# Down products and projection of a first layer as token rows instead of transposed sums, with its bias added on GpSimd and the recurrence begun one pair of chunks sooner

## The chip, the cores and the metric

One core of a Trainium2 chip. The time is device time of one execution of the kernel, in microseconds (us), as the median of three runs. Lower is better.

## The reference

Input is `x` of 4 sequences of 512 tokens, 256 wide; on the chip the tokens are taken in blocks of 128 per sequence, so that 4 blocks of 4x128 tokens make up the work. Two layers follow each other, each a mixer and a mixture of experts beside it, added to the residual:

```python
xn = _layernorm(x)
x = x + _L0_attn_ref(xn, w_qkv, w_proj, b_proj) + _L0_ffn_ref(xn, ...)
xn = _layernorm(x)
x = x + _L1_attn_ref(xn, W_in, b_in, W_out, b_out, gamma, beta) + _L1_ffn_ref(xn, ...)
```

- First mixer: linear attention in 8 heads. `q` and `k` pass a relu, `v` is padded with a column of ones, `vk = v_pad k^T` is summed over all tokens of a sequence, `vk q` is divided by its last row, and `@ w_proj.T + b_proj` closes it.
- First mixture: 16 experts of 176 hidden units, the top 6 by softmax for each token. The kernel computes all 2,816 hidden units for all tokens, in 22 chunks of 128, and multiplies each by the token's weight for its expert, which is 0 for the ten others.
- Second mixer: a recurrence over the 512 tokens, `s = tanh(u_t + s * gamma + beta)` with 512 hidden values, where `u = xn @ W_in.T + b_in`; its states go through `W_out`.
- Second mixture: 8 experts of 176 hidden units, the top 2 for each token with weights that sum to 1, and a shared expert of 352 hidden units.

## The kernel before

Matrices are split in a head and a tail in float16, and a product is three matmuls (`PRODUCTS`: head by head, tail by head, head by tail) into one float32 sum. TensorE's unit of work is a matmul of 128x128 weights with 512 moving columns: 4 sequences x 128 tokens.

**Stages.** A prologue makes the first norm, the attention's sums over tokens and the first pieces of weights. Then come four phases, one for each block of tokens, in which the 22 chunks of the dense mixture pass in 11 pairs (`pair(k, ...)`, `PAIRS`). For each chunk TensorE makes the gate product into bank G, the up product into a bank of U (6 matmuls each), and the down product of the chunk two before (`down`, L1020, 6 matmuls) into the two banks Y of the phase's parity. ScalarE makes the silu (L1328) and the head of the hidden units (`hh`, L1336), VectorE multiplies (L1845) and weighs (L1851), GpSimd makes the tail (`hl`, L1984). G is one bank, so the gate of the next chunk waits for the silu of this one.

**Side work.** Each engine runs a written list. `stages(phase)` gives two tables: `front[k]`, side work that stands in front of pair k, and `woven[k]`, parts that VectorE puts between its own operations of pair k. So, in phases 1 to 3, for the block before: the sums leave the banks (front 1 and 2), the second layer's norm is woven into pairs 2 and 3, `norm_turn` transposes its result (front 4), `logits` stands in front 5, the products `inputs` with `W_in` in fronts 5 and 6 (constants `INPUT_A`, `INPUT_B`). For the own block, `project` (`w_proj`, L848 on) adds to the same sums (front 2).

**Sums of the first layer.** `down` has weights as the stationary operand and hidden units as the moving one, so its sum has the features on partitions and tokens along the columns: `Y[j % 2][dh]`, half `dh` of the features. Before the sums can be added to the residual `xres`, which has tokens on partitions, ScalarE copies them with scale and bias to `yT` (`sum_copy`, L1242), TensorE transposes 8 squares of 128 (`sum_turn`, L889) and VectorE adds (L1697).

**The recurrence.** It runs beside all this: a step is a scan on VectorE (L1830) and a tanh on ScalarE (L1368), each waiting for the other. From `FIRST_TICK` of phase 1 on, a pair carries 12 steps (`STEPS`). Its inputs are copied from the banks into the buffer RING by ScalarE (`input_copy`, L1263). In the first phases RING also holds staged pieces of the second layer's weights, of which `PAIR_PIECES` gives the pair: (1, 2) holds pieces 38 to 41. When piece 40, the last of the sorted gate and up weights, is done on ScalarE (heads, L1205) and VectorE (tails, L1491, L1493), SP issues the DMA that parks them in DRAM (`park`, L709), behind loads of later pieces (`load_down`, L684). `input_copy(0, 0)` and `input_copy(1, 0)` wait for a parking:

```python
def input_copy(j, c, bank_):
    act.wait_ge(u_done, KH * j + c + 1)
    if j < 2 and c == 0:
        act.wait_ge(parked_out[j], 16)
```

**The units.** Behind the phases come 35 units (`UNITS`): 3 of the shared expert, 23 of pairs of tiles with tokens sorted by expert, 9 shared. `UNIT_STEPS` says how many steps of the recurrence each carries, `UNIT_FRONT`, `UNIT_GAPS` and `UNIT_WOVEN` what side work: the last block's sums and norm among the first, its routing and scatter after, and from unit 18 the gathers of routed results (L2033) with stores of tiles (L2052) on GpSimd's queue.

## Time and profile before

| | |
|---|---|
| three runs, median (lowest to highest) | 658.88 us (658.23 to 660.16) |
| profiled execution, span from first to last instruction | 655.6 us |
| profiled execution, its own time | none recorded beside the span |
| TensorE, matmuls, busy | 610.9 us |
| VectorE busy | 447.3 us |
| ScalarE busy | 366.1 us |
| GpSimd busy | 239.1 us |
| mean granted clock of TensorE | 0.990 |

The span does not hold what lies before the first instruction and after the last. Of the stages, phases 0 to 3 begin at about 55, 152, 258 and 360 us, the units at about 460. Engines are named PE (TensorE), PEld (its weight loads), DVE (VectorE), ACT (ScalarE), POOL (GpSimd) and SP (SyncE). Two consecutive starts of a row of matmuls tell the time of one better than the column of durations, which overlap. A bracket at the end of a row gives the idle time of the engine ahead of it, and what ended it.

### The profile page before, as it was taken

To read this page: it belongs to the slowest core of one execution; us is meant where nothing else is said; L and a number is where in the kernel's file an instruction comes from. 1 tells how busy PE (TensorE), PEld (TensorE's weight loads), DVE (VectorE), ACT (ScalarE), POOL (GpSimd) and SP (SyncE) were. 2 spreads that over 40 slices of the span, in tenths; PEclk is the share of its full clock that TensorE was granted. 3 is DMA by queue.
4 is the path that set the end of the run, shared out by engine and by line. 5 is a ranking of instruction groups with operands and counts; after the bars stand their busy time and mean duration, and the time that the engine had idled before them with its cause. 6 is when DMAs were issued, how large, how long until landed. Compare 5 with 4: busy or idle time off the path is not lost. (4 is left out here: it accounts for less than half of the span.)

```text
span 655.6 us, 12530 instructions
## 1 busy us (share of the span) xinstructions
PE 610.9 (93%) x3579; PEld 338.7 (52%) x3579; DVE 447.3 (68%) x1526; ACT 366.1 (56%) x1004; POOL 239.1 (36%) x256
## 2 busy tenths in 40 slices
PE   5999899999999999999999989999979989777997
PEld 2665444544444444444454434454446667556675
DVE  7983967667862677776478696477676666676677
ACT  2446345456546446657755657754546765663561
POOL 5246222132242225524224533222542361374371
PEclk8999999999999999999999999999998999999999
DMA  8203667872386452855346650324512445563143
GB/s 298 80 1 105 224 222 252 274 237 78 112 325 216 140 185 84 270 194 192 127 155 202 217 179 30 128 94 71 112 51 66 101 135 115 129 174 110 66 129 97
DMA packets 89548, 97.99 MB, mean 149 GB/s; under 512 B 29375, under 2 KB 80159, under 8 KB 89055
## 3 DMA queue, kind: packets, MB, share of 16 engines
q10 hardware_dynamic: 45472, 46.01, 21.4%
q1 hardware_dynamic: 38734, 36.82, 19.1%
q0 software_dynamic: 5280, 14.42, 7.0%
q8 instruction: 29, 0.48, 0.3%
q14 instruction: 33, 0.26, 0.1%
HBM read 27.96 MB, written 63.24 MB: 139 GB/s over the span
## 5 line engine op out<-in xcount | busy, mean ns | idle before, releaser
L1984 POOL TENSOR_TENSOR hl<-scr,hh 128x512 f16<-128x512 f32 (+2 forms) x91 | 105.3, 1157 | 276.6 <-ACT hh L1336 276.6
L1368 ACT ACTIVATE RING<-zbuf 128x16 f32<-128x16 f32 x512 | 110.9, 217 | 148.5 <-DVE zbuf L1830 143.5
L762 PE MATMUL G<-xT,W 128*128 128x512 f16 (+2 forms) x600 | 145.9, 379 | 8.2 <-ACT scr L1328 5.7
L762 PE MATMUL U<-xT,W 128*128 128x512 f16 (+2 forms) x600 | 145.8, 379 | 2.8 <-DVE scr L1845 2.8
L1830 DVE TENSOR_TENSOR_SCAN zbuf<-C,RING 128x32 f32<-128x32 f32 x354 | 77.8, 220 | 75.0 <-ACT RING L1368 74.6
L762 PEld LDWEIGHTS U<-xT,W 128*128 128x128 f16 (+3 forms) x600 | 60.9, 102 | 71.9 <-DVE scr L1845 4.3
L762 PEld LDWEIGHTS G<-xT,W 128*128 128x128 f16 (+3 forms) x600 | 60.1, 102 | 73.1 <-issue 6.4
L1020 PE MATMUL Y<-hh,W 128*128 128x512 f16 x352 | 90.3, 379 | 0.0
L1851 DVE TENSOR_TENSOR U<-U,CS 128x512 f32<-128x512 f32 x88 | 60.4, 686 | 38.6 <-PE U L762 31.9
L1328 ACT ACTIVATE scr<-G 128x512 f32<-128x512 f32 (+2 forms) x100 | 58.9, 589 | 45.0 <-PE G L762 44.5
L1336 ACT ACTIVATE hh<-scr 128x512 f16<-128x512 f32 (+2 forms) x100 | 61.8, 618 | 29.1 <-DVE scr L1845 28.9
L1845 DVE TENSOR_TENSOR scr<-scr,U 128x512 f32<-128x512 f32 (+2 forms) x100 | 67.4, 674 | 3.0 <-PE U L762 0.9
L1020 PEld LDWEIGHTS Y<-hh,W 128*128 128x128 f16 (+1 forms) x352 | 34.4, 98 | 41.5 <-issue 0.3
L1020 PE MATMUL Y<-hl,W 128*128 128x512 f16 x176 | 52.4, 379 | 0.3 <-POOL hl L1984 0.2
L1830 DVE TENSOR_TENSOR_SCAN zbuf<-gam,RING 128x32 f32<-128x32 f32 x158 | 35.6, 225 | 24.6 <-ACT RING L1368 24.2
L2052 POOL DMA_DIRECT2D yrows<-scr x46 | 25.7, 559 | 59.1 <-issue 58.5
L2033 POOL DMA_INDIRECT W<-yrows,row_id x32 | 34.0, 1061 | 11.2 <-issue 6.7
L2020 POOL DMA_INDIRECT xrows<-XR,row_id x32 | 34.4, 1074 | 8.0 <-issue 7.7
L762 PE MATMUL Y<-xT,W 128*128 128x512 f16 x144 | 33.2, 379 | 1.8 <-DVE gexp L1516 1.8
L1020 PEld LDWEIGHTS Y<-hl,W 128*128 128x128 f16 (+1 forms) x176 | 16.6, 98 | 22.3 <-POOL hl L1984 3.7
L952 PE MATMUL U<-W,xT 128*128 128x512 f16 x96 | 25.0, 399 | 2.7 <-DVE W L1503 2.7
L1503 DVE SCALAR_TENSOR_TENSOR W<-stage,W 128x768 f16<-128x768 f32 (+1 forms) x21 | 20.6, 1003 | 7.4 <-ACT W L1183 7.0
(204 smaller groups left out, 839.5 us busy)
## 6 DMA issues: line engine op xcount, KB each, us to landing
xrows<-zeros ACTq DMA_DIRECT2D x13, 1280.0 KB, 5.7
yrows<-zeros ACTq DMA_DIRECT2D x10, 1536.0 KB, 6.0
stage<-weights SPq DMA_DIRECT2D x20, 384.0 KB
yrows<-zeros ACTq DMA_DIRECT2D x5, 1408.0 KB, 6.0
yrows<-scr POOLq DMA_DIRECT2D x46, 128.0 KB
xrows<-zeros ACTq DMA_DIRECT2D x5, 1152.0 KB, 5.4
stage<-weights SPq DMA_DIRECT2D x14, 256.0 KB
parked<-RING SPq DMA_DIRECT2D x1, 3520.0 KB, 12.0
```

The source lines that it names most:

```text
L762: last = nc.tensor.matmul(bank_, w(wp), act(ap), start=start and n == 0, stop=stop and n == count - 1)
L1020: last = nc.tensor.matmul(Y[j % 2][dh][:, :], weight(CHUNK0 + c, wp, 2 * KD * P + dh * P), act[ap][:, a, :], start=start and m == 0, stop= ...
L1328: nc.scalar.activation(sg[a][rows, :], G[rows, :], ACT.Silu, scale=1.0 / W_SCALE).then_inc(silu_done, 1)
L1336: nc.scalar.activation(hh[rows, a, :], h32[a][rows, :], ACT.Copy).then_inc(hhead_done, 1)
L1368: nc.scalar.activation(RING[:, (t + 1) % RING_T, ::2], zbuf[:, 1::2], ACT.Tanh).then_inc(state_done, 1)
L1830: nc.vector.tensor_tensor_scan(zbuf[:, :], held_gamma if held else gam[:, :], RING[:, t % RING_T, :], 0.0, ALU.mult, ALU.add)\
L1845: nc.vector.tensor_tensor(h32[a][rows, :], sg[a][rows, :], U[a][rows, :], ALU.mult).then_inc(gated_done, 1)
L1851: nc.vector.tensor_tensor(U[a][:, :], U[a][:, :], spread_slot(phase), ALU.mult).then_inc(weighed_done, 1)
L1984: nc.gpsimd.tensor_tensor(hl[rows, a, :], h32[a][rows, :], hh[rows, a, :], ALU.subtract)\
L2020: nc.gpsimd.indirect_dma_start(xrows, bass.IndirectOffsetOnAxis(row_id[:, j, b, k:k + 1], 0), XR[:, b, :], None).then_inc(scattered, 16)
L2033: nc.gpsimd.indirect_dma_start(YG[:, i % RING_YG, :], None, yrows, bass.IndirectOffsetOnAxis(row_id[:, j, b, k:k + 1], 0))\
L2052: nc.gpsimd.dma_start(yrows[DS(row, P), :], yT[r % 2][:, t * DIM:(t + 1) * DIM])\
```

## The change

- `down` and `project` exchange the operands: 128 tokens of hidden units are stationary and 256 features of the weights move. A down is 12 matmuls of 256 columns for 6 of 512; the sums are rows of tokens, the halves of `Y[j % 2][b // 2]` for sequence b.
- `sum_copy` and `sum_turn` go. `sum_part` on VectorE scales a bank and adds it to `xres`, woven into pair 1.
- The bias of the projection is written by SP as one row to DRAM and loaded to all partitions; GpSimd adds it to the 16 tiles of `xres`, two in front of each of pairs 1 to 8 of phase 0.
- `project` moves from front 2 to front 1; norm, `norm_turn`, `logits`, `exp` and `inputs` each move one pair sooner, and `FIRST_TICK` from 7 to 6. So 27 in place of 26 pairs carry steps, and `UNIT_STEPS` sums to 188 in place of 200: units 14 to 25 have 6 steps for 7, and the side work of units 2 to 12 moves one unit sooner.
- `PAIR_PIECES`, `park` and the wait in `input_copy` are as before.

```diff
-UNIT_STEPS = (6, 6, 6, 4, 4, 4, 6, 6, 6, 6, 6, 6, 7, 7, 7, 7, 7, 7, 7, 7, 7, 7, 7, 7, 7, 7, 6, 6, 6, 6, 6, 6, 0, 0, 0)
+UNIT_STEPS = (6, 6, 4, 4, 4, 6, 6, 6, 6, 6, 6, 6, 7, 7, 6, 6, 6, 6, 6, 6, 6, 6, 6, 6, 6, 6, 6, 6, 6, 6, 6, 6, 0, 0, 0)
...
-        FIRST_TICK = 7
+        FIRST_TICK = 6
...
-        SUM_COPY, SUM_TURN, NORM, NORM_TURN, INPUT_A, INPUT_B = 1, 2, 2, 4, 5, 6
-        LOGITS, EXP, ROUTE, RANK, TABLE, SCATTER, SPREAD = 5, 6, 7, 9, 10, 10, 10
+        ADD_SUMS, NORM, NORM_TURN, INPUT_A, INPUT_B = 1, 1, 3, 4, 5
+        LOGITS, EXP, ROUTE, RANK, TABLE, SCATTER, SPREAD = 4, 5, 7, 9, 10, 10, 10
-        O_TURN, PROJECT = 0, 2
+        O_TURN, PROJECT = 0, 1
+        BIAS = range(1, 9)
...
+            sp.wait_ge(bias_parked, 16)
+            sp.dma_start(proj_bias, bias_row.broadcast_to([P, DIM])).then_inc(bias_loaded, 16)
             with sp.Fori(EARLY // 2 + 1, SLOTS // 2) as r:
...
-                for dh in range(KD):
-                    split_product(pair[dh][:, :], [
-                        (lambda p_, h=h: W[:, MISC, p_, h * DIM + dh * P:h * DIM + (dh + 1) * P],
-                         lambda p_, h=h: oT[:, h, p_, :]) for h in range(2)], start=False, stop=False)
+                for b in range(BATCH):
+                    for h in range(2):
+                        for m, (wp, ap) in enumerate(PRODUCTS):
+                            nc.tensor.matmul(pair[b // 2][:, b % 2 * DIM:(b % 2 + 1) * DIM], oT[:, h, ap, b * P:(b + 1) * P],
+                                             W[:, MISC, wp, h * DIM:(h + 1) * DIM],
+                                             start=j > 0 and b % 2 == 0 and h == 0 and m == 0, stop=False,
+                                             skip_group_check=True)
...
-                    for dh in range(KD):
+                    for b in range(BATCH):
                         for m, (wp, ap) in enumerate(PRODUCTS):
                             if ap == part:
-                                last = nc.tensor.matmul(Y[j % 2][dh][:, :], weight(CHUNK0 + c, wp, 2 * KD * P + dh * P),
-                                                        act[ap][:, a, :], start=start and m == 0,
-                                                        stop=stop and ap == 1)
+                                last = nc.tensor.matmul(
+                                    Y[j % 2][b // 2][:, b % 2 * DIM:(b % 2 + 1) * DIM], act[ap][:, a, b * P:(b + 1) * P],
+                                    W[:, DS(CHUNK0 + c, 1), wp, 2 * KD * P:PIECE].rearrange("p o n -> p (o n)"),
+                                    start=start and b % 2 == 0 and m == 0, stop=stop and ap == 1, skip_group_check=True)
...
-            def sum_turn(phase, pair):
-
-                for half in range(2):
-                    dve.wait_ge(y_turned, 2 * phase + half + 1)
+            def sum_part(phase, part):
+
+                if part in (1, 2):
+                    if part == 1:
+                        dve.wait_ge(down_done, (phase + 1) * CH0)
+                        dve.wait_ge(bias_added, BATCH * BLOCKS)
+                    half = part - 1
                     rows = xres[:, phase, 2 * half:2 * half + 2, :]
-                    nc.vector.tensor_tensor(rows, rows, pair[half][:, :].rearrange("p (b d) -> p b d", b=2), ALU.add)\
+                    nc.vector.scalar_tensor_tensor(out=rows, in0=Y[phase % 2][half][:, :].rearrange("p (b d) -> p b d", b=2),
+                                                   scalar=Y_DESCALE, in1=rows, op0=ALU.mult, op1=ALU.add)\
                       .then_inc(x_added, 1)
...
+            def bias(first):
+
+                if first == 0:
+                    pool.wait_ge(bias_loaded, 16)
+                    pool.wait_ge(xn_done, BATCH * BLOCKS)
+                for i in (first, first + 1):
+                    nc.gpsimd.tensor_tensor(xres[:, i // BATCH, i % BATCH, :], xres[:, i // BATCH, i % BATCH, :], proj_bias,
+                                            ALU.add).then_inc(bias_added, 1)
```

The order on TensorE in phase 0, a chunk's gate and up products and the down product of two chunks before, in the kernel before (Y00 and Y01 are the two banks, and the last number of a row is how many follow each other):

```order
L762 MATMUL G<-xT,W 128x512 x6
L762 MATMUL U0<-xT,W 128x512 x6
L1020 MATMUL Y00<-hh,W 128x512 x2
L1020 MATMUL Y01<-hh,W 128x512 x2
L1020 MATMUL Y00<-hl,W 128x512
L1020 MATMUL Y01<-hl,W 128x512
```
There a bank holds a half of the features and takes three products of 512 tokens. In the changed one it is this:

```order
L776 MATMUL G<-xT,W 128x512 x6
L776 MATMUL U0<-xT,W 128x512 x6
L1026 MATMUL Y00<-W,hh 128x256 x4
L1026 MATMUL Y01<-W,hh 128x256 x4
L1026 MATMUL Y00<-W,hl 128x256 x2
L1026 MATMUL Y01<-W,hl 128x256 x2
```
Gate and up products are as before; each bank holds two sequences and takes six products of 256 features, with the hidden units as the stationary side.

The order on ScalarE in phase 1, from behind the last part of piece 41 (pair 2's last) to the copies of the inputs (`RING<-Y,ubias`), in the kernel before; `xT<-Y` and `XR<-scr` are the norm's copies, `xrows<-zeros` a DMA that fills rows:

```order
L1328 ACTIVATE scr<-G 128x512
L1336 ACTIVATE hh<-scr 128x512
L1328 ACTIVATE scr<-G 128x512
L1336 ACTIVATE hh<-scr 128x512
L1215 ACTIVATE xT<-Y 128x512 x2
L1251 ACTIVATE XR<-scr 128x4x256
L1286 DMA xrows<-zeros 128x10x512
L1328 ACTIVATE scr<-G 128x512
L1336 ACTIVATE hh<-scr 128x512
L1328 ACTIVATE scr<-G 128x512
L1336 ACTIVATE hh<-scr 128x512
L1263 ACTIVATE RING<-Y,ubias 128x4x128 x2
```
Two pairs of chunks stand there between the pieces and the copies of the inputs. In the changed one, with the last heads of pieces as the first two rows, the order is this:

```order
L1212 ACTIVATE RING<-stage 128x4x8x7
L1212 ACTIVATE RING<-stage 128x4x40
L1222 ACTIVATE xT<-Y 128x512 x2
L1252 ACTIVATE XR<-scr 128x4x256
L1287 DMA xrows<-zeros 128x10x512
L1329 ACTIVATE scr<-G 128x512
L1337 ACTIVATE hh<-scr 128x512
L1329 ACTIVATE scr<-G 128x512
L1337 ACTIVATE hh<-scr 128x512
L1264 ACTIVATE RING<-Y,ubias 128x4x128 x2
```
One pair of chunks (four rows of silu and head) fewer stands between the pieces and the copies, and the copies now precede the silu that begins pair 4.

The order on VectorE in phase 1 from the second chunk of pair 1 on, in the kernel before, the rows with `RING<-stage` being tails of pieces:

```order
L1845 TENSOR_TENSOR scr<-scr,U 128x512
L1851 TENSOR_TENSOR U<-U,CS 128x512
L1491 SCALAR_TENSOR_TENSOR RING<-stage,RING 128x8x13 x4
L1493 SCALAR_TENSOR_TENSOR RING<-stage,RING 128x4x24
L1491 SCALAR_TENSOR_TENSOR RING<-stage,RING 128x8x13 x4
L1493 SCALAR_TENSOR_TENSOR RING<-stage,RING 128x4x24
L1697 TENSOR_TENSOR xres<-xres,Y 128x512 x2
L1446 BN_STATS stats<-xres 128x6
L1845 TENSOR_TENSOR scr<-scr,U 128x512
L1446 BN_STATS stats<-xres 128x6 x3
```
The additions come there behind the tails of pair 1, in pair 2. In the changed one, from the first chunk of pair 1 on, the order is this:

```order
L1861 TENSOR_TENSOR scr<-scr,U 128x512
L1701 SCALAR_TENSOR_TENSOR xres<-Y,xres 128x512 x2
L1447 BN_STATS stats<-xres 128x6 x2
L1867 TENSOR_TENSOR U<-U,CS 128x512
L1447 BN_STATS stats<-xres 128x6
L1492 SCALAR_TENSOR_TENSOR RING<-stage,RING 128x8x13 x4
L1494 SCALAR_TENSOR_TENSOR RING<-stage,RING 128x4x24
L1492 SCALAR_TENSOR_TENSOR RING<-stage,RING 128x8x13 x4
L1494 SCALAR_TENSOR_TENSOR RING<-stage,RING 128x4x24
L1447 BN_STATS stats<-xres 128x6
```
The sums' additions (`xres<-...`) and the norm's first parts (`BN_STATS`) stood behind all tails of pair 1's pieces and now stand ahead of them.

## Rows read from the trace of the kernel before

**Rows 1.** The page, part 1: busy us, share of span, instructions.
```profile
PE 610.9 (93%) x3579; PEld 338.7 (52%) x3579; DVE 447.3 (68%) x1526; ACT 366.1 (56%) x1004; POOL 239.1 (36%) x256
```

**Rows 2.** Timeline of TensorE, phase 1: start us, us, what, [idle before].
```profile
188.83 1.46 PE L762 MATMUL G<-xT,W 128*128 128x512 f16 x6
...
192.71 1.46 PE L762 MATMUL G<-xT,W 128*128 128x512 f16 x6
...
196.60 0.94 PE L786 MATMUL Y<-W,xT 128*128 128x8 f16 x32
...
199.99 1.24 PE L762 MATMUL G<-xT,W 128*128 128x512 f16 x5
```

**Rows 3.** Timeline of TensorE, phase 3, the attend's products.
```profile
437.98 5.40 PE L875 MATMUL Y<-W,SH 128*128 128x256 f16 x48
443.22 0.59 PE L762 MATMUL G<-xT,W 128*128 128x512 f16 x2
```

**Rows 4.** Timeline of TensorE, phase 1, transposes and projection.
```profile
168.03 1.04 PE L889 MATMUL Y<-cst,scr 128*128 128x128 f32 x8
168.90 2.75 PE L762 MATMUL Y<-scr,W 128*128 128x512 f16 x12
```

**Rows 5.** Timeline of ScalarE, phase 1, the inputs' copies.
```profile
199.50 1.14 ACT L1263 ACTIVATE RING<-Y,ubias 128x512 f32<-128x512 f32 x1 [4.17 <-DMA parked<-RING]
...
201.48 0.60 ACT L1328 ACTIVATE scr<-G 128x512 f32<-128x512 f32 x1
```

**Rows 6.** Timeline of SP, phase 1, DMA issues.
```profile
183.66 3.70 SPq L684 DMA_DIRECT2D stage<-weights  x7
187.41 0.36 SPq L709 DMA_DIRECT2D parked<-RING  x1
```

**Rows 7.** The page, part 6: DMA issues, KB each, median us to landing.
```profile
parked<-RING SPq DMA_DIRECT2D x1, 3520.0 KB, 12.0
```

**Rows 8.** Timeline of VectorE, phase 1, first tail of piece 40.
```profile
183.55 0.59 DVE L1491 SCALAR_TENSOR_TENSOR RING<-stage,RING 128x56 f16<-128x56 f32 x4
```

**Rows 9.** Timeline of TensorE, phase 3, its two waits.
```profile
393.86 1.47 PE L762 MATMUL G<-xT,W 128*128 128x512 f16 x6 [2.30 <-ACT scr L1328]
...
410.77 1.47 PE L762 MATMUL Y<-xT,W 128*128 128x512 f16 x6 [1.84 <-DVE gexp L1516]
```

**Rows 10.** Timeline of ScalarE, phase 3, two splits of states.
```profile
389.72 2.06 ACT L1272 ACTIVATE SH<-RING 128x512 f16<-128x512 f32 x2 [0.22 <-ACT RING L1368]
```

**Rows 11.** Timeline of VectorE, phase 3, two steps of the recurrence.
```profile
406.33 0.22 DVE L1830 TENSOR_TENSOR_SCAN zbuf<-C,RING 128x32 f32<-128x32 f32 x1 [0.28 <-ACT RING L1368]
406.84 0.22 DVE L1830 TENSOR_TENSOR_SCAN zbuf<-C,RING 128x32 f32<-128x32 f32 x1 [0.28 <-ACT RING L1368]
```

**Rows 12.** Timeline of TensorE, unit 3, the transposes of the last sums.
```profile
479.53 1.09 PE L889 MATMUL Y<-cst,scr 128*128 128x128 f32 x8 [0.41 <-ACT scr L1242]
```

**Rows 13.** Two stretches: length, busy by engine (PE first), PEclk, DMA, GB/s.
```profile
486.00:490.00 4.00, 2.47 (x14) 1.52 (x15) 3.65 (x18) 0.62 (x4) 1.17 (x1) 0.88 0.42 102
490.00:493.00 3.00, 3.00 (x17) 2.05 (x16) 1.92 (x8) 1.49 (x7) 0.00 (x0) 0.59 0.00 0
```

**Rows 14.** Timeline of TensorE, unit 21, its first routed products.
```profile
576.27 1.14 PE L1105 MATMUL Y<-W,CS 128*128 x6 [0.79 <-DVE scr L1863]
```

**Rows 15.** Timeline of GpSimd, units 21 and 22, the first store of each.
```profile
576.23 0.58 POOL L2052 DMA_DIRECT2D yrows<-scr  x1 [0.38 <-issue]
...
580.80 0.58 POOL L2052 DMA_DIRECT2D yrows<-scr  x1
```

**Rows 16.** Waits of TensorE in phase 1: us in total, times, longest us.
```profile
PE G L762 <- ACT scr L1328: 2.3, 3, 1.1
```

**Rows 17.** Timeline of GpSimd, phase 0, a tail of hidden units.
```profile
73.60 1.15 POOL L1984 TENSOR_TENSOR hl<-scr,hh 128x512 f16<-128x512 f32 x1 [2.00 <-ACT hh L1336]
```

**Rows 18.** Timeline of VectorE, phase 0, two casts beside it.
```profile
73.26 0.20 DVE L1537 CAST cw<-grest 128x64 bf16<-128x64 f32 x1
...
73.75 1.06 DVE L1535 CAST cw<-grest 128x64 bf16<-128x64 f32 x1
```

More of the change, by code:

```diff
@@ L413, in stages @@
             elif 1 < phase:
-                front[FIRST_TICK].append(("more_inputs", (phase,)))
+                tick, step_ = divmod(P * (phase - 1), STEPS)
+                woven[tick - tick_of(phase, 0)].append(("late_inputs", (phase, 1 - step_)))
+                assert tick == tick_of(phase, INPUT_B) and step_ > 0
             return front, woven
@@ L648, in _ @@
             load_x(3)
+            with nc.allow_non_contiguous_dma(reason="one row of 256"):
+                sp.dma_start(bias_row.rearrange("o (h n) -> o h n", h=KD),
+                             vectors[:, 3 * KH:3 * KH + KD].rearrange("(o n) h -> o h n", o=1)).then_inc(bias_parked, 16)
             for s in range(CHUNK0, EARLY):
```

96 lines of the change are left out of this document (47 added, 49 removed).

## The prediction

> **What bounds the kernel now.** I read the page first: TensorE is busy 610.9 us of a span of 655.6, 93%, VectorE 68% [rows 1]. So a change of this kernel counts by what it adds to TensorE's stream or takes from it, and by TensorE's idle time, about 45 us, which I then looked up in its waits. The four phases, in which 22 chunks of hidden units pass in 11 pairs, run solid but for a few short waits; the units behind them wait often, a little each. The reader is to see three places. In phase 1 ScalarE stood 4.17 us before the recurrence's first inputs, because their buffer was still being parked, and TensorE did not notice [rows 5]. In phase 3 TensorE waited 2.30 us behind the split of the states and 1.84 us behind a softmax [rows 9]. Among the units the last block's sums and norm stand in the way: where they pass, TensorE works 2.47 of 4 us [rows 13], and its transposes waited 0.41 [rows 12].
>
> The three runs have a median of 658.88 us, 3.3 above the span of the profiled execution, and spread over 1.9 us. I make the sum against the span and add it to the median. A difference under 0.3%, 2.0 us, cannot be told from none here.
>
> **Down products as token rows.** From the start of one gate product to that of the next lie 18 matmuls of 512 columns in 3.88 us, 215.6 ns each [rows 2]. The 48 products of 256 columns of the attend take 5.24 us, 109.2 ns each [rows 3], so the weight load of each was covered there. Six of the one become twelve of the other: 1.310 against 1.294 us, 16 ns more for each of 88 chunks, **+1.4**. The four projections, 12 to 24 each, add 0.03 us apiece, **+0.1**. The bounds are 0 and +2.8, twice this.
>
> **Transposes of sums.** The eight stand in phase 1 from 168.03 to 168.90, 0.87 us [rows 4], and as long in phases 2 and 3: **−2.6**. The fourth set, among the units, goes with the units' term. ScalarE's two copies and VectorE's adds lay beside TensorE; the add remains, with a scale, on VectorE, one pair sooner.
>
> **Bias.** The row goes through DRAM on SP's queue, ahead of loads which wait for a free stage buffer anyhow; without that cover two issues cost those loads 0.7 us, at 0.36 for one of SP's [rows 6]. No compute waits for the row before the first addition. Sixteen additions of 128x256 on GpSimd: a 128x512 one there took 1.15 us [rows 17], so I estimate 0.6 us each by half its size, two in front of a pair's tail products, in a phase in which GpSimd waits for ScalarE. They lie hidden there, unless VectorE suffers. One small cast of VectorE took 1.06 us, beginning 0.15 us after GpSimd's operation of 1.15 us and ending with it, to 0.06 [rows 17, 18]. That is contention in a pair of engines whose later products TensorE waits for. I take **+0.4**, between 0 and 1.3.
> The Trainium skill (SBUF — State Buffer, "Who interferes with whom") says that VectorE and GpSimd share a port pair which one instruction locks as a whole, and that an operation of VectorE with two SBUF inputs is held by one of GpSimd that reads SBUF; this row agrees with it, and by that rule the sixteen additions are a cost, of which the last rival gives the limit.
>
> **Inputs of the recurrence, one pair sooner.** This is the largest term, and it is positive. The buffer that the copies write, RING, also holds pieces of weights, which SP parks in DRAM. The table that times those pieces is not changed, nor the wait of the copy for the parking. The parking has seven loads ahead of it on SP, which begin at 183.66, when piece 40 is done by VectorE [rows 6, 8]; it is issued at 187.41 and needs 12.0 us [rows 6, 7], so it lands at 199.4, and the copy began at 199.50 [rows 5]. In the kernel before the copies stand in front of pair 5, whose first gate begins at 199.99 [rows 2]; TensorE had its second gate still to wait for and was done with the first only at 203.9, so the next silu, begun at 201.48, came in time. Now they stand in front of pair 4. The piece is still the last of pair 2 on VectorE, with about as much work ahead of it (the sums and the norm move from after it to before it, the transposes go), so I put the landing at 199.2, the copies to 201.4, and the silu of pair 4's first chunk to 202.0. TensorE wants to begin that pair's second gate, which needs this silu, at 192.71, plus logits and inputs that now stand ahead of it (196.60 to 199.99, 3.4), less 0.87 of transposes [rows 2, 4]: 195.2. It waits 202.0 − 195.2 = 6.8, of which I take **+6.7**. The order of the copies does not let silu pass: ScalarE works its own list from the top. A part of it may be spent a pair earlier, since the piece's head parts stand directly before ScalarE's next group; that moves the wait, not its end. Lower bound +4.2: VectorE sheds all the idle third of a pair of 7.8 us (68% busy) ahead of the piece, 2.5 us. Upper bound +8.9, about as far the other way, if VectorE is that much later with the piece.
>
> **One pair more with steps of the recurrence.** Steps share ScalarE with the silu. In the last four pairs of phase 1, the ones with steps, TensorE waited for silu three times, 2.3 us in all, 1.1 the longest [rows 16]; one of the pairs did not wait. The new one comes while no norm is woven, and I take **+0.3** (0 to 1.0).
>
> **Phase 3.** The norm's transposed copies move from the front of pair 4 to that of pair 3, where half the state splits already stand: 2.06 us for two on ScalarE [rows 10]. The wait of 2.30 there [rows 9] is behind these splits. The copies of the norm, of the same size, 2.1 us by the splits' duration, now come first: 4.4. In pair 2 the other two splits had the projection's 2.6 us beside them, which moves to pair 1; of their 2.06 I put 1.1 on TensorE. The later 1.84, a softmax behind a late piece of weights, I put at 0.5, because the softmax is a pair sooner now. 6.0 against 4.14: **+1.8**, with bounds −1.8 (the former wait in pair 3, none in pair 2, the 1.84 gone) and +3.5 (the 1.84 as before, and 0.3 more in pair 2).
>
> **Units 2 to 13.** The sums' copy, the transposes with their 0.41 of wait [rows 12] and a unit's wait for the norm go. With the norm done one unit sooner I come to the sixth unit's gate 3.3 us sooner: **−3.3** (−0.9, the transposes alone, to −5).
>
> **Units 14 to 25.** Twelve steps of the recurrence fewer, one in each unit. A step takes 0.51 us from scan to scan [rows 11], so at most −6. TensorE waits at the start of such a unit for VectorE, which has the steps in its list [rows 14]. But in units 19 to 23 GpSimd issues its stores and gathers without a pause, 4.57 us from unit to unit [rows 15]; there the steps may not be what is last. I give the first five units their 2.5 us, and the others 1.5 together: **−4.0** (−1 to −6).
>
> **Clock.** Where TensorE worked little it then ran at a low clock: 0.59 granted on average over 490 to 493 us, so mostly at 1.2 GHz, after those 4 us in which it was busy for 2.47 [rows 13]. Of three microseconds a part of 0.41 is lost, 1.2 us. Two new waits longer than any in the phases before, times half a chance: **+0.7** (0 to 2.8).
>
> **Sum**: 1.5 − 2.6 + 0.4 + 6.7 + 0.3 + 1.8 − 3.3 − 4.0 + 0.7 = +1.5. On the median: **660.4 us**, no difference that can be measured.
>
> **Rivals.** *The units give all of it.* Steps set the pace up to unit 25 (−6) and the norm moves the full −5, the parking as forecast: 3.7 less than the sum, −2.2, 656.7; with the parking's lower bound also 2.5 less, 654.2. For it: TensorE's waits in the units are for VectorE, among steps [rows 14]. Against it: GpSimd's unbroken row. *GpSimd holds the units*, so the steps taken out give nothing there beyond 1 us: +3 on the sum, 663.4. It decides if gathers of unit 18 onward start no sooner than before. *The parked write costs the clock*: this one ends slower. TensorE stands in pair 4 of phase 1 until the copies are through, at the upper bound of 8.9 (2.2 more than taken), and takes up work at 1.2 GHz for about 3 us, there and after the wait in pair 3 of phase 3: 2 x 1.2, of which 0.7 is counted. That is +3.9 on the sum, 664.3. It decides from the point at which a wait lasts so long that the granted clock falls. The 2.30 of phase 3 [rows 9] is the longest in the phases before, and the new ones are two and three times as long. *GpSimd's additions hold VectorE.* At the price of the one cast, 1.06 against 0.20 for its neighbour [rows 18], each addition delays VectorE by 0.9, 14 us in all; half of it reaching TensorE, which VectorE's slack speaks against, gives 7 in place of 0.4: 667.0. *The change does not do what it says*: were weight loads not covered at 256 columns, every down product would be longer; the attend shows them covered, so I give it nothing.
>
> **How the numbers follow.** Forecast 0.38; the units give all 0.26, faster; GpSimd holds the units 0.15; clock and parking 0.18; additions 0.03. So faster 0.26, no change 0.38, slower 0.36. The range leaves one in ten on either side: down to 654.5, near the fast case with the parking's lower bound, and up to 665.5, past the case of the clock but not that of the additions.
>
> **What would show it.** In the profile of the changed kernel, the copy of the inputs on ScalarE should wait for the parked write some 8 us or more, with a TensorE wait of 5 to 7 us behind silu in pair 4 of phase 1; transposes of sums gone; a down of 12 products in 1.31 us; units 14 to 18 shorter by half a microsecond. The prediction is wrong if the parking lands before TensorE asks for the second gate of pair 4, or if units 19 to 23 too become shorter.

## The result, and the profile after

The changed kernel takes **667.49 us** in the median of four runs (665.09 to 670.45), against 658.56 for the kernel before; the ratio is 1.0146 with an interval of 1.0108 to 1.0185. It is slower by about 9 us, outside the forecast range of 654.5 to 665.5. The profiled execution took 670.45 us, its span is 668.8; the spans of the other runs are 663.4 to 667.9, and in the four runs the mean granted clock is 0.976, 0.976, 0.982 and 0.986, the slower the lower. The ledger below is of the profiled execution, the slowest, so its difference of 13.2 us is some 4 more than that of the medians. Of all the runs behind the times of this document, one of experiment 8 took 2,235.86 us, over three times the others, and is left out of that kernel's time.

The page's line of busy times, which answers to [rows 1]; TensorE's busy time grew by 6.2 us, though the transposes are gone:

```profile
PE 617.1 (92%) x4123; PEld 392.7 (59%) x4123; DVE 451.4 (67%) x1526; ACT 360.7 (54%) x996; POOL 256.8 (38%) x272
```

From one gate product to the same one in both traces, the 13.2 us between the spans fall apart like this; the forecast is the sum of those terms that belong to a stage, but for the clock. The units begin at 466.73 us in the kernel before and at 482.59 in the changed one. The column for the clock is TensorE's time lost while its granted clock was half, as read from windows of the profile; the kernel's time can lose less (experiment 1).

| stage | before | after | difference | of it clock at half, after less before | forecast without clock |
|---|---|---|---|---|---|
| to the first chunk | 55.80 | 56.28 | +0.5 | 0 | 0 |
| phase 0 | 96.69 | 98.04 | +1.35 | 0 | +0.75 |
| phase 1 | 105.87 | 115.64 | +9.8 | +2.6 | +6.5 |
| phase 2 | 102.38 | 102.69 | +0.3 | 0 | −0.5 |
| phase 3 | 105.99 | 109.94 | +3.95 | +2.8 | +1.3 |
| units 0 to 13 | 76.91 | 76.81 | −0.1 | −0.8 | −3.3 |
| units 14 to 24 | 57.22 | 54.06 | −3.2 | 0 | −4.0 |
| unit 25 to the end | 54.74 | 55.34 | +0.6 | +1.7 | 0 |

**Phase 1.** ScalarE's timeline, which answers to [rows 5]:

```profile
202.50 1.11 ACT L1264 ACTIVATE RING<-Y,ubias 128x512 f32<-128x512 f32 x1 [11.70 <-DMA parked<-RING]
...
204.29 0.63 ACT L1329 ACTIVATE scr<-G 128x512 f32<-128x512 f32 x1
```

SP's timeline, which answers to [rows 6], and from the DMA view of 184 to 204 us the parking's size and time to landing, as in [rows 7]:

```profile
185.72 4.84 SPq L698 DMA_DIRECT2D stage<-weights  x7
190.60 0.35 SPq L723 DMA_DIRECT2D parked<-RING  x1
```

```profile
parked<-RING SPq DMA_DIRECT2D x1, 3520.0 KB, 11.8
```

TensorE's timeline there, with waits in pairs 3 and 4:

```profile
188.18 1.47 PE L776 MATMUL G<-xT,W 128*128 128x512 f16 x6 [2.61 <-ACT scr L1329]
...
204.98 2.74 PE L776 MATMUL G<-xT,W 128*128 128x512 f16 x6 [5.44 <-ACT scr L1329]
207.52 2.77 PE L776 MATMUL U<-xT,W 128*128 128x512 f16 x6
210.08 1.16 PE L1026 MATMUL Y<-W,hh 128*128 128x256 f16 x8
```

ScalarE has waited 11.70 us for the parked write, and TensorE 5.44 us for the silu behind it, where 6.8 was worked out. The gate product behind this wait lasts 2.54 us from start to start in place of 1.30. That is the clock:

**The clock.** Three stretches of the changed kernel, behind the waits in phase 1, phase 3 and unit 3 (columns: length, busy by engine, granted clock, DMA share, GB/s):

```profile
204.98:210.08 5.10, 5.10 (x13) 1.79 (x14) 0.67 (x1) 2.76 (x4) 2.28 (x2) 0.50 0.47 155
409.49:414.58 5.09, 5.09 (x12) 1.79 (x13) 2.99 (x11) 3.05 (x13) 1.16 (x1) 0.50 0.00 0
498.81:503.90 5.09, 5.09 (x20) 3.02 (x21) 4.44 (x18) 1.46 (x7) 2.69 (x3) 0.50 0.14 52
```

The granted clock is 0.50, 1.2 GHz, while TensorE is busy all the time, and ahead of each it had been idle for 3.8 to 5.4 us. In phase 1 the twelve gate and up products took 5.10 us for 2.59, and the rest of the stretch lost a little more.

**Phase 3.** TensorE's timeline, which answers to [rows 9]; the wait for the softmax is gone:

```profile
396.28 1.47 PE L776 MATMUL G<-xT,W 128*128 128x512 f16 x6 [1.35 <-ACT scr L1329]
...
409.49 2.74 PE L776 MATMUL G<-xT,W 128*128 128x512 f16 x6 [3.85 <-ACT scr L1329]
412.02 2.77 PE L776 MATMUL U<-xT,W 128*128 128x512 f16 x6
```

**Units.** TensorE's first routed products (unit 3), VectorE and ScalarE ahead of them:

```profile
498.81 3.70 PE L1112 MATMUL U<-W,BD 128*128 x12 [3.81 <-DVE scr L1861]
502.30 1.06 PE L1078 MATMUL Y<-W,hh 120*128 120x256 f16 x4
```

```profile
493.88 1.26 DVE L1701 SCALAR_TENSOR_TENSOR xres<-Y,xres 128x512 f32<-128x512 f32 x2
...
495.32 0.72 DVE L1447 BATCH_NORM_STATS2 stats<-xres 128x6 f32<-128x256 f32 x2
...
497.85 0.69 DVE L1861 TENSOR_TENSOR scr<-scr,U 112x512 f32<-112x512 f32 x1
```

```profile
496.54 0.60 ACT L1329 ACTIVATE scr<-G 112x512 f32<-112x512 f32 x1
```

The last block's sums now stand on VectorE ahead of two steps of the recurrence, ScalarE has these steps ahead of its silu of unit 2, and TensorE waits 3.81 us for the product with that silu. In the kernel before it waited 1.19:

```profile
481.82 1.96 PE L1105 MATMUL U<-W,BD 128*128 x12 [1.19 <-DVE scr L1845]
```

### The profile page after: what moved, and what is told of

Same layout as the page of the kernel before. It is cut to its first block and busy times, and to the rows that moved or that the text cites. A ratio compares the mean times of both kernels' runs of the same rounds, so it can differ in the third digit from the quotient of the medians.

```text
span 668.8 us, 13609 instructions
## 1 busy us (share of the span) xinstructions
PE 617.1 (92%) x4123; PEld 392.7 (59%) x4123; DVE 451.4 (67%) x1526; ACT 360.7 (54%) x996; POOL 256.8 (38%) x272
## 5 line engine op out<-in xcount | busy, mean ns | idle before, releaser
L776 PE MATMUL G<-xT,W 128*128 128x512 f16 (+2 forms) x600 | 149.1, 385 | 19.3 <-ACT scr L1329 17.3
L776 PE MATMUL U<-xT,W 128*128 128x512 f16 (+2 forms) x600 | 149.7, 386 | 3.2 <-DVE scr L1861 3.1
L1846 DVE TENSOR_TENSOR_SCAN zbuf<-C,RING 128x32 f32<-128x32 f32 x364 | 80.1, 220 | 74.7 <-ACT RING L1367 74.2
L1026 PE MATMUL Y<-W,hh 128*128 128x256 f16 (+1 forms) x704 | 91.7, 273 | 0.1
L1026 PEld LDWEIGHTS Y<-W,hh 128*128 128x128 f16 x704 | 69.1, 98 | 27.9 <-issue 1.7
L1026 PE MATMUL Y<-W,hl 128*128 128x256 f16 (+1 forms) x352 | 52.9, 273 | 0.3 <-POOL hl L2000 0.2
L1846 DVE TENSOR_TENSOR_SCAN zbuf<-gam,RING 128x32 f32<-128x32 f32 x148 | 32.9, 222 | 24.0 <-ACT RING L1367 23.8
L1026 PEld LDWEIGHTS Y<-W,hl 128*128 128x128 f16 x352 | 33.9, 98 | 5.5 <-POOL hl L2000 1.1
L1112 PE MATMUL U<-W,BD 128*128 x108 | 20.7, 334 | 8.4 <-DVE scr L1879 4.4
## 6 DMA issues: line engine op xcount, KB each, us to landing
parked<-RING SPq DMA_DIRECT2D x1, 3520.0 KB, 11.8
```

The costliest lines, as they stand in the source:

```text
L776: last = nc.tensor.matmul(bank_, w(wp), act(ap), start=start and n == 0, stop=stop and n == count - 1)
L1026: last = nc.tensor.matmul(Y[j % 2][b // 2][:, b % 2 * DIM:(b % 2 + 1) * DIM], act[ap][:, a, b * P:(b + 1) * P], W[:, DS(CHUNK0 + c, 1), wp ...
L1846: nc.vector.tensor_tensor_scan(zbuf[:, :], held_gamma if held else gam[:, :], RING[:, t % RING_T, :], 0.0, ALU.mult, ALU.add)\
```

## Experiments

**1. Does the clock cost what its windows show?** Products are put into TensorE's waits; nothing reads their sums.

```diff
+            FILL = {(1, 4, 1): 24, (3, 3, 1): 16}
...
                     for a in range(2):
+                        if isinstance(k, int) and (phase, k, a) in FILL:
+                            n = phase * CH0 + 2 * k + a
+                            pe.wait_ge(gated_done, n - 1)
+                            for m in range(FILL[phase, k, a]):
+                                nc.tensor.matmul(U[a][:, :], weight(CHUNK0, 0, 0), xT[:, phase, 0, 0, :],
+                                                 start=True, stop=True)
                         gate_up(phase, 2 * k + a, a)
```

> The changed kernel with 24 products of 512 columns put ahead of the second gate of pair 4 in phase 1 (where TensorE waited 5.44 us) and 16 ahead of the second gate of pair 3 in phase 3 (3.85 us); their sums are overwritten. They last 5.2 and 3.5 us, less than the waits. Theory, the clock: the waits stay as long by the start of those gates, but the gate product behind each takes 1.30 us in place of 2.54, and the profile is 2.7 + 2.8 = some 5.5 us shorter than that of the changed kernel, 668.8. Rival, the half clock there comes from something else than the idle time: the slow products stay, and the time is the same within 1 us.

TensorE's timeline in phase 1 and 3 of this kernel:

```profile
199.14 5.34 PE L1040 MATMUL U<-xT,W 128*128 128x512 f16 x24
204.44 1.47 PE L776 MATMUL G<-xT,W 128*128 128x512 f16 x6
205.75 1.46 PE L776 MATMUL U<-xT,W 128*128 128x512 f16 x6
```

```profile
406.13 6.28 PE L1040 MATMUL U<-xT,W 128*128 128x512 f16 x16 [3.69 <-DVE scr L1868]
412.25 1.46 PE L776 MATMUL G<-xT,W 128*128 128x512 f16 x6
```

Phase 1 came out as the theory says: the gate behind the filling starts when silu allows it and lasts 1.31 us, and from that gate to pair 6 it is 14.30 us for 16.92, 2.6 less. In phase 3 the test failed by its own making: the filling waits for the product that frees its bank, which came only after a wait of 3.69 us, so it filled nothing, ran at the low clock itself (16 products in 6.12 us) and put the gate back. The time is 667.72 us (ratio to before 1.0122 to 1.0226), no gain; the span of its profile is 664.9.

The units of this kernel are those of the changed one, with the same wait in unit 3, and their clock stayed up. Units 0 to 13 took 75.18 us here, and 75.18 in experiment 8 too, for 76.81; from unit 25 to the end it is 53.66 for 55.34. So the stretch at unit 3 cost the kernel 1.6 us, where its window shows 2.5 lost by TensorE, and that of unit 26 cost 1.7. The clock's price is shown for phase 1 and the units; for phase 3 it rests on the windows.

**2. The parking ahead of the loads.**

```diff
-            load_down(DOWN_PIECE)
             park(0, DOWN_PIECE, spare[:, 0:parked[0].shape[1]])
+            load_down(DOWN_PIECE)
```

> The changed kernel with the parking issued ahead of the seven loads of the next piece on SP's queue. Theory, the parked write bounds pair 4: the issue comes at 186.6 for 190.6, the landing and the inputs' copies 4.0 us sooner, TensorE's wait in pair 4 falls from 5.44 to about 1.5 and the clock does not fall there: 4.0 + 2.7 = 6 to 7 us less in all. Rival, the silu in pair 4 is held by ScalarE's own list or by the transfer's share of the DMA engines with the loads: the landing comes less than 2 us sooner, and under 2 us are gained.

Page row of the parking, and ScalarE's copy:

```profile
parked<-RING SPq DMA_DIRECT2D x1, 3520.0 KB, 14.2
```

```profile
202.17 1.11 ACT L1264 ACTIVATE RING<-Y,ubias 128x512 f32<-128x512 f32 x1 [10.10 <-DMA parked<-RING]
```

The transfer was issued at 187.89, in a phase 1 that began 1.3 us later than in the changed kernel, so 4.0 us sooner by that; but it took 14.2 us for 11.8, and 1.6 are left at the landing. Loads stand behind it on its queue in both kernels. What is new beside it is a write of zeros from ScalarE's queue (`xrows<-zeros`, 1,280 KB), issued at 186.39 and landed 5.2 us later; in the changed kernel this write (185.11, 5.8 us) had all but landed when the parking was issued. From 186 to 192 us ScalarE's queue moved 1.31 MB and SP's 0.45. TensorE's wait in pair 4 is 3.83 us for 5.44, the clock falls behind it here too, and from pair 4's second gate to pair 6 it is 15.98 us for 16.92. Phase 1 is 2.6 us shorter in all. The time is 666.05 us, ratio to before 1.0078 to 1.0140. The rival is nearer for the landing, under 2 us sooner: the parked write does bound pair 4, but its own speed beside that write gives back a good part of what the queue gives.

**3. The splits of the states sooner**, in phase 3.

```diff
-        FIRST_SPLIT, FIRST_ATTEND = (2, 2, 3, 3), 8
+        FIRST_SPLIT, FIRST_ATTEND = (0, 1, 1, 2), 8
```

> The changed kernel with the four splits of the states of block 0 in fronts 0, 1, 1 and 2 of phase 3 in place of 2, 2, 3, 3. Theory, splits and norm copies in one front make the wait: the waits of 1.35 and 3.85 us in pairs 2 and 3 go to under 1.5 together, and the half clock behind the second goes: 3.5 + 2.8 = about 6 us less. Rival, they only move with the splits to pairs 0 and 1, where the projection covers one of them: waits of 2 us or more there, and a gain under 3 us.

TensorE's two waits left there:

```profile
396.22 1.47 PE L776 MATMUL G<-xT,W 128*128 128x512 f16 x6 [1.74 <-ACT scr L1329]
...
406.41 1.47 PE L776 MATMUL G<-xT,W 128*128 128x512 f16 x6 [0.77 <-ACT scr L1329]
```

No wait is left in pairs 0 and 1, the clock stays up, and from the start of phase 3 to pair 6 it is 60.81 us for 65.49: 4.7 less. The wait in pair 2 stays, with one split where there were two. The time is 664.15 us, ratio to before 1.0061 to 1.0111.

**4. Units 2 to 12 as before**, one unit later.

```diff
-            2: [("scatter", (2, 3)), ("sums", (3,))],
-            4: [("norm_turn", (7, Y[1]))],
-            5: [("shared_add", (0, Y[0])), ("logits", (7, Y[1][1]))],
...
+            2: [("scatter", (2, 3))],
+            3: [("sums", (3,))],
+            5: [("shared_add", (0, Y[0])), ("norm_turn", (7, Y[1]))],
+            6: [("logits", (7, Y[1][1]))],
...
```

> The changed kernel with the side work of units 2 to 12 (last sums, norm, routing) one unit later, as in the kernel before, with steps 6, 6, 6, 4, 4, 4 in the first units; steps of units 14 to 25 as changed. Theory, the sums in front of unit 2 delay its two steps and so its silu: the wait of 3.81 us at the first routed product falls to about 1.2, the half clock behind it goes or comes later, and units 3 to 13 are 2 to 4 us shorter. Rival, the norm one unit sooner is worth what was forecast, 3.3 us: this kernel is as slow or slower than the changed one.

The wait at the first routed product is 2.16 us for 3.81. But from the gate of unit 2 (484.68) to unit 14 it is 67.9 us, with a stretch at half clock of its own, against 68.5 for the changed kernel, and 66.9 for the kernel of experiment 1, whose units ran at full clock. At full clock units 0 to 13 took 75.18 us with the earlier norm (experiments 1 and 8) and 74.48 with the old order (experiment 10). So the norm one unit sooner gains nothing here and loses 0.7 us: what it saves ahead it waits for at unit 3. Both sides missed. The time is 665.95 us, ratio 1.0094 to 1.0185.

**5. Token rows and bias with the old timetable.** Side work, units and steps are those of the kernel before.

```diff
-        FIRST_TICK = 6
+        FIRST_TICK = 7
-        ADD_SUMS, NORM, NORM_TURN, INPUT_A, INPUT_B = 1, 1, 3, 4, 5
-        LOGITS, EXP, ROUTE, RANK, TABLE, SCATTER, SPREAD = 4, 5, 7, 9, 10, 10, 10
+        ADD_SUMS, NORM, NORM_TURN, INPUT_A, INPUT_B = 2, 2, 4, 5, 6
+        LOGITS, EXP, ROUTE, RANK, TABLE, SCATTER, SPREAD = 5, 6, 7, 9, 10, 10, 10
-        O_TURN, PROJECT = 0, 1
+        O_TURN, PROJECT = 0, 2
...
```

> The changed kernel with the timetable of the kernel before: sums, norm, routing, inputs, projection and FIRST_TICK at their old pairs, units and their steps as before; down products and projection as token rows, no transposes and the bias on GpSimd stay. Theory, the loss comes from the earlier timetable and not from the other form of the sums: waits of the kernel before return, none of 5.44 in phase 1, no half clock in the phases, and the time is within 3 us of the kernel before, by +1.6 for products, -3.5 for transposes, +1.0 for the bias some 1 us below it. Rival, products of 256 columns and the bias on GpSimd cost more than the rows of phase 0 show: 4 us or more above the kernel before.

This kernel leaves the first two chunks out of the sums of phases 1 to 3: they are multiplied, but the projection starts the sum anew behind them. It takes 658.03 us, a ratio of 0.9960 to 1.0012: the time of the kernel before. **All of the loss is in the earlier timetable**; experiment 10, which sums all chunks in the old order, comes to the same time. The form of the sums alone gives nothing back either: phases 0 to 3 are 1.4, 0.9, 0.6 and 0.3 us longer than in the kernel before, though three sets of transposes (2.6 us) are gone. Behind this stand the bias (1.05, experiment 7), the products and some new short waits, in phase 1 for VectorE (0.34 and 1.05 for 0.75) and in phase 2 for silu (0.64); the units are about as much shorter.

**6. The copies of the first inputs behind the silu of pair 4.**

```diff
-                front[INPUT_A].append(("inputs", (phase - 1, 0, other)))
+                if phase == 1:
+                    front[INPUT_A].append(("inputs_pe", (phase - 1, 0, other)))
+                    front[INPUT_A + 1].append(("inputs_act", (phase - 1, 0, other)))
+                else:
+                    front[INPUT_A].append(("inputs", (phase - 1, 0, other)))
```

> The changed kernel, in which ScalarE copies the first inputs of phase 1 in front of pair 5, after the silu of pair 4, and TensorE makes the products in front of pair 4 as changed. Theory, it is the place in ScalarE's list that makes TensorE wait for the parked write: the wait of 5.44 us at the second gate of pair 4 goes, one of under 2 us comes ahead of the next inputs' products, the clock stays up: 3.5 + 2.7 = some 6 us less than the changed kernel. Rival, the wait only moves, since the next products need the same banks: 4 us or more there.

TensorE waits here instead, at the next inputs' products. ScalarE's copies ahead of them still wait for the parked write, and a write of zeros is issued sooner:

```profile
207.23 2.75 PE L780 MATMUL Y<-xT,W 128*128 128x512 f16 x12 [2.56 <-issue]
```

```profile
189.45 0.38 ACTq L1291 DMA_DIRECT2D xrows<-zeros  x1
...
205.13 2.00 ACT L1268 ACTIVATE RING<-Y,ubias 128x512 f32<-128x512 f32 x2 [0.38 <-DMA parked<-RING]
```

2.56 us for 5.44, without a fall of the clock. A shorter stretch at half clock came behind the wait of pair 3 in its place (2.36 us there). It delayed TensorE by some 1.7 us, estimated from the granted clock of the four microseconds from 189 on, 0.53, 0.50, 0.50 and 0.76, so that without it the wait would have been about 4.2, which is the rival's. To pair 6 it is 4.0 us less than in the changed kernel, not 6; with the 2.6 of the clock taken off, 1.4. The edit also moved the landing. In the changed kernel ScalarE issues this write of zeros, 1,280 KB, with its first copy, at 202.55; here it ran beside the parking (issued at 190.15), which took 14.9 us for 11.8. So this kernel does not show what the place in the list costs by itself. The time is 665.49 us, ratio 1.0051 to 1.0168.

**7. The bias later.**

```diff
-        BIAS = range(1, 9)
+        BIAS = range(3, 11)
```

> The changed kernel with the bias additions in front of pairs 3 to 10 of phase 0 in place of 1 to 8. Theory, the additions hold VectorE where it is late anyhow, in pairs 1 and 2: TensorE's waits there go back from 2.15 and 0.92 us to 1.64 and 0.41, and phase 0 is 1.0 us shorter, with nothing lost in pairs 9 and 10. Rival, the waits grew by something else (the copy of the bias row, other placement), and stay.

TensorE's waits in pairs 1 and 2 of phase 0, in the changed kernel and in this one:

```profile
70.77 1.47 PE L776 MATMUL U<-xT,W 128*128 128x512 f16 x6 [2.15 <-DVE scr L1861]
...
80.53 1.47 PE L776 MATMUL U<-xT,W 128*128 128x512 f16 x6 [0.92 <-DVE scr L1861]
```

```profile
69.95 1.47 PE L776 MATMUL U<-xT,W 128*128 128x512 f16 x6 [1.63 <-DVE scr L1861]
...
79.19 1.47 PE L776 MATMUL U<-xT,W 128*128 128x512 f16 x6 [0.39 <-DVE scr L1861]
```

What the additions hold are the tails of weight pieces on VectorE, which read two tensors, in pair 1 of the changed kernel and of this one:

```profile
64.98 2.69 DVE L1504 SCALAR_TENSOR_TENSOR W<-stage,W 128x768 f16<-128x768 f32 x2 [0.82 <-ACT W L1190]
```

```profile
64.69 2.15 DVE L1504 SCALAR_TENSOR_TENSOR W<-stage,W 128x768 f16<-128x768 f32 x2 [0.82 <-ACT W L1190]
```

0.54 us, as much as TensorE's wait falls there (0.52). Over phase 0 the twenty tails are hardly shorter here (23.7 us for 24.0; 19.5 in the kernel before): they are held later, where TensorE does not wait for them. Phase 0 is 96.99 us for 98.04: 1.05 less, as expected to the tenth, and 0.3 more than before, which the products account for. The time is 665.98 us, ratio 1.0052 to 1.0161.

**8. Steps put back in units 14 to 25.**

```diff
-UNIT_STEPS = (6, 6, 4, 4, 4, 6, 6, 6, 6, 6, 6, 6, 7, 7, 6, 6, 6, 6, 6, 6, 6, 6, 6, 6, 6, 6, 6, 6, 6, 6, 6, 6, 0, 0, 0)
+UNIT_STEPS = (6, 6, 4, 4, 4, 6, 6, 6, 6, 6, 6, 6, 7, 7, 7, 7, 7, 7, 7, 7, 7, 7, 7, 7, 7, 7, 4, 4, 4, 4, 4, 4, 0, 0, 0)
```

> The changed kernel with 7 steps again in units 14 to 25 and 4 for 6 in units 26 to 31. Theory, steps set the pace of units 14 to 19 and GpSimd's row of stores and gathers that of units 20 to 24: from the start of unit 14 to that of unit 20 it is some 2.5 us longer than the changed kernel (25.4 us), from 20 to 25 the same within 0.5 (28.7 us). Rival 1, GpSimd sets both: no difference in either. Rival 2, steps set both: 2.5 to 3 us longer in each.

TensorE's first products of units 14, 20 and 25, of the changed kernel and of this one:

```profile
559.40 1.06 PE L1112 MATMUL U<-W,CS 128*128 x6
...
584.84 1.07 PE L1112 MATMUL U<-W,BD 128*128 x6 [0.81 <-DVE scr L1879]
...
613.46 0.76 PE L1112 MATMUL U<-W,CS 128*128 x4
```

```profile
556.80 1.06 PE L1112 MATMUL U<-W,CS 128*128 x6
...
584.74 1.07 PE L1112 MATMUL U<-W,BD 128*128 x6 [0.79 <-DVE scr L1879]
...
613.23 1.06 PE L1112 MATMUL U<-W,CS 128*128 x6
```

To unit 20: 25.44 and 27.94 us, 2.5 more. From there to unit 25: 28.62 and 28.49. The theory holds in both; either rival would show in one of them. (In the kernel before it is 28.12 and 29.10.) This kernel had two stretches at half clock here, from about 574 and 595 us, which the changed one had not; units 17 and 19, outside them, are 0.8 and 0.4 us longer by themselves, and unit 18, inside the first, took 5.29 us where the kernel before took 5.22 at full clock. The time is 670.21 us, ratio 1.0123 to 1.0248.

**9. The parking by halves**, ahead of the loads, each with its semaphore; the first inputs wait for the half they overwrite.

```diff
-            load_down(DOWN_PIECE)
-            park(0, DOWN_PIECE, spare[:, 0:parked[0].shape[1]])
+            half = RING_T * 2 * BATCH * KH
+            sp.wait_ge(pieces_split, DOWN_PIECE)
+            sp.dma_start(parked[0][:, 0:half], spare[:, 0:half]).then_inc(parked_half, 16)
+            sp.dma_start(parked[0][:, half:], spare[:, half:parked[0].shape[1]]).then_inc(parked_out[0], 16)
+            load_down(DOWN_PIECE)
...
-                if j < 2 and c == 0:
-                    act.wait_ge(parked_out[j], 16)
+                if j == 0 and c == 0:
+                    act.wait_ge(parked_half, 16)
+                if j == 1 and c == 0:
+                    act.wait_ge(parked_out[0], 16)
+                    act.wait_ge(parked_out[1], 16)
```

> The changed kernel with the parking issued ahead of the next piece's loads, as two transfers, the half that the first inputs overwrite first; the copy waits for that half alone, every other reader and writer for both. Theory, the parked write is what TensorE waits for in pair 4: 1,835 KB of the half at the rate of the whole (3,520 KB in 11.8 us) need about 6.2 us, so it lands near 193, before TensorE's inputs' products are done at 195.5, and the wait of 5.44 us and the half clock behind it go: 8 us less than the changed kernel in phase 1. Rival, the transfers share the engines so that the first half lands late: a wait of over 3 us stays.

ScalarE's copy, and TensorE's second gate of pair 4, of this kernel:

```profile
196.25 1.15 ACT L1274 ACTIVATE RING<-Y,ubias 128x512 f32<-128x512 f32 x1 [4.65 <-DMA parked<-RING]
```

```profile
198.87 1.04 PE L1032 MATMUL Y<-W,hh 128*128 128x256 f16 x8
199.74 0.60 PE L1032 MATMUL Y<-W,hl 128*128 128x256 f16 x4
200.18 1.46 PE L782 MATMUL G<-xT,W 128*128 128x512 f16 x6
```

The half that matters is 2,048 KB (the expectation had 1,835) and took 8.8 us, so it landed at 196.2 and not at 193; TensorE did not wait for it all the same. Phase 1 is 107.50 us for 115.64: 8.1 less, as expected. The time is 659.18 us, ratio to before 1.0007 to 1.0057, and at most 0.6% above it where the changed kernel was 1.5%.

**10. Rows with the old order, mended.** Experiment 5 with all chunks summed, with the edits of experiments 3 and 7.

```diff
-                                             start=j > 0 and b % 2 == 0 and h == 0 and m == 0, stop=False,
+                                             start=False, stop=False,
...
-                            first = phase == 0 and isinstance(k, int) and (k, a) == (1, 0)
+                            first = isinstance(k, int) and (k, a) == (1, 0)
```

> Token rows and bias with the timetable of the kernel before, all chunks summed, bias in front of pairs 3 to 10, splits of the states in fronts 0, 1, 1, 2 of phase 3. Theory: 656.7 of the profile with rows only, less 1.05 for the bias and some 2 for the splits' waits (1.83 and 0.77), so about 653.5 in the profile, 0.3 to 0.6% below the kernel before. Rival, the softmax and the units take back what the splits give: the same time as the kernel before.

658.81 us, ratio 0.9980 to 1.0022: the rival. The bias is 1.05 cheaper, but the splits' waits came back in pairs 0 and 1 (0.49 and 2.08 us, and a stretch at half clock behind the second), where with the old order no projection stands beside them.

**11. The earlier timetable, mended**: experiments 3, 7 and 9 together, and the copy to XR one pair later in phase 1.

```diff
-                front[NORM_TURN].append(("rows", (phase - 1, 0)))
-                front[NORM_TURN + 1].append(("rows", (phase - 1, 1)))
+                front[NORM_TURN + (phase == 1)].append(("rows", (phase - 1, 0)))
+                front[NORM_TURN + 1 + (phase == 1)].append(("rows", (phase - 1, 1)))
```

> The changed kernel with its earlier timetable kept and its waits mended: parking by halves ahead of the loads, the first block's copy to XR one pair later, splits in fronts 0, 1, 1, 2, bias in front of pairs 3 to 10. Theory: 668.8 less 8 in phase 1, 5 in phase 3, 1 in phase 0 and 1 at pair 3, so about 654 in the profile, at or just below the kernel before; the earlier start itself is worth about 3 us, in units 14 to 20, given back in part at unit 3. Rival, the earlier timetable costs more than is seen: 658 or more.

The page's busy times, and from its waits of TensorE the largest in total and the longest single one:

```profile
PE 609.8 (93%) x4119; PEld 390.2 (60%) x4123; DVE 452.9 (69%) x1526; ACT 361.0 (55%) x996; POOL 257.8 (39%) x272
```

```profile
PE G L782 <- ACT scr L1339: 9.6, 11, 1.7
...
PE U L1118 <- DVE scr L1871: 3.8, 1, 3.8
```

**654.08 us** in the median, ratio to before 0.9924 to 0.9964: faster than both kernels, by 0.6% and by 2%. The wait in pair 3 fell from 2.61 to 1.63 us; one of 1.44 us is left in pair 4. The 3.8 us at unit 3 are still there. What is won over the kernel before stands in units 14 to 24, 53.78 us for 57.22; phase 1 is still 2.2 us longer (108.04).

## Why the prediction was wrong

- **The parked write: mechanism right, size inside its bounds.** +6.7 was taken for phase 1's wait. With the 2.6 of the clock taken off, the phase lost 7.2 us where all its terms gave 6.5. The wait is split as the text allowed: 2.61 in pair 3, where the norm's copies stand directly behind the piece's heads on ScalarE, and 5.44 in pair 4, 8.05 together. The landing came at 202.4, 1.4 us later than forecast once the later start of phase 1 (1.8) is taken off. Experiment 9 shows the cause: with the half it needs parked first, the wait of pair 4 is gone. Neither of the two signs that the prediction names for being wrong came: the parking landed long after TensorE asked, and units 19 to 23 are as long as before (23.94 us for 23.97).
- **The step that failed first: the clock, "+0.7".** The term gives the two new waits half a chance at a price of 1.2; by these words it should have been 1.2, and it was put at 0.7. The clock fell behind both waits, and again in unit 3 and in unit 26, and TensorE lost 2.6, 2.8, 2.5 and 1.7 us by it, against 3.3 in the kernel before: **+6.3** by the windows in this execution. In the kernel's time the stretch at unit 3 cost 1.6 (experiment 1), and those of the kernel before some 1.6 too, estimated as its 76.91 us for units 0 to 13, less 0.87 for transposes, less the 74.48 of experiment 10 at full clock; that makes about +7. The price of 1.2 was read from three microseconds; the low clock lasted at least five in phase 1, phase 3 and unit 3. The run with a mean clock of 0.986 has a span of 663.4 for 668.8. That its low clock cost less fits this, but where its clock fell is not known.
- **The step that failed second: "units 2 to 13, −3.3".** Units 0 to 13 are 0.1 us shorter as they stand. At full clock the earlier norm makes them 0.7 us longer (75.18 for 74.48), which uses up most of the 0.87 of transposes. I had followed the norm to the logits, and not what stands behind it on VectorE: the sums ahead of two steps, the steps ahead of silu, silu ahead of TensorE. The stage misses its forecast by 3.2 us, whatever the clock does in the others.
- **Phase 3, +1.8: right.** 1.35 + 3.85 for 2.30 + 1.84; 1.1 and 4.4 were forecast. Without the clock the phase is 0.15 us from the sum. Experiment 3 shows that the splits beside the norm's copies make it.
- **Units 14 to 25, −4.0: right in kind, 0.8 too much.** −3.2, of which −2.7 before unit 20; experiment 8 shows steps as the pace up to there and not behind it. The rival in which GpSimd holds the units was too strong.
- **Products of 256 columns, +1.5: right.** The last chunk of phase 3 in the changed kernel, which waits for nothing, has its gate, up and down in 3.90 us (478.69 to 482.59) for 3.88.
- **Bias, +0.4: 1.05**, inside its bounds. The additions were estimated at 0.6 us and took 1.44 in the median. In GpSimd's row of the changed kernel (columns: shortest, median and longest ns, first and last start):

```profile
L2045 POOL TENSOR_TENSOR xres<-xres,SH x16: 725/1438/1458, 65.4 to 129.3; 128x256 f32<-128x256 f32 x16
```

The shortest, 0.73, is near the estimate; most are twice that, and VectorE is late where they run. What VectorE does there are the tails of pieces, `W<-stage,W`, which read two tensors in SBUF and took 2.69 us for 2.15. This is the hold that the Trainium skill (SBUF — State Buffer, "Who interferes with whom") describes for an instruction of VectorE with two SBUF inputs beside one of GpSimd that reads SBUF; experiment 7 prices it at 0.5 us for each of two pairs. The row of the prediction does not show that part of the rule: it was a cast, with one input.
- **One pair more with steps, +0.3: nothing.** TensorE's waits in the last pairs of phase 1 are those of the kernel before (0.36, 0.80 and 1.07 us for silu, for 0.41, 0.82 and 1.08).
- **Phase 2, new:** a wait of 0.63 us for silu in pair 3, which no term had. Experiments 5 and 10 have it too (0.64 and 0.63), so it does not come from the earlier timetable.
- **The rivals.** What came is nearest to "the parked write costs the clock", 664.3, which had 0.18: its mechanism, but with four falls of the clock rather than two, and with no gain from the norm to set against it.

## What to carry to other kernels

When a stage is moved ahead, look for what it waits for beside the engines: here a buffer's last user was a 12 us transfer whose issue had not been moved, and the copy that waited for it stood ahead of everything else in its engine's list. Let a wait cover only the bytes it protects; half of the parking was enough. On TensorE, price a new wait of some microseconds as the wait and often a stretch at half clock behind it (at unit 3 in seven of nine kernels), and look for several small waits in place of one long one. When a list is reordered, see which transfers of other queues it lets go sooner: in experiment 6 a write of zeros came forward beside the awaited transfer, which took 3 us longer.

## What the runs showed that was not expected

- A transfer of 3,520 KB took 11.8 us in the changed kernel, 14.2 in experiment 2 and 14.9 in experiment 6, with loads behind it on its queue each time. In the latter two a write of 1,280 KB from another queue, issued shortly before it, ran beside it; so 4.0 us sooner on the queue became 1.6 at the landing.
- The same wait does not always cost the clock. Ahead of unit 3's twelve products TensorE waited 3.8 us in the changed kernel and in that of experiment 1; they took 3.49 us in the one (498.81 to 502.30), and in the other, in the row below, 1.98. What decides it stays open. Of the nine kernels with these units in this order (the changed one and experiments 1, 2, 3, 6, 7, 8, 9 and 11) seven had the stretch there. In phase 0 the changed kernel's wait of 2.15 us left the clock up; in experiments 2, 3 and 9, with the same products up to there, it fell behind that wait, and phase 0 became 0.6 us longer (98.6 for 98.04).

```profile
498.77 1.98 PE L1119 MATMUL U<-W,BD 128*128 x12 [3.79 <-DVE scr L1868]
```

- Additions on GpSimd of 128x256 in float32 took longer in the median (1.44 us) than its operation of 128x512 that writes float16 (1.16), in the same phase.
- Left open: what the wait of 3.8 us at unit 3 would give back. Silu ahead of the steps in unit 2 was not tried.
